# A group's update in three pieces and roots for three groups at once, in the weighted sum of a graph network kernel

## What is computed

```python
dst = (6250 * uniform(100000) ** 2.0).astype(int32)   # sorted; src is sorted along
edge_index = stack([src, dst])
h = maximum(_layernorm(x), 0.0)                       # (x - m) / sqrt(v + eps)
# attention, _L0: score from q[dst], k[src]; e = exp(score - smax[dst])
ssum = segment_sum(e, dst)
m = v[src] * attn[:, :, None]                         # attn = e / ssum[dst]
t = segment_sum(m, dst).reshape(N, DIM)
new_h = (t @ Wa + ba) * alpha + h * (1.0 - alpha)
x = x + new_h
h = maximum(_layernorm(x), 0.0)                       # input of the next layer
# _L1: four message layers; _L2: two convolutions; _L3: a linear layer with neighbours
```

## Time and profile before

| what | us |
|---|---|
| median of 3 runs | 10655.52 (10635.86 to 10660.82) |
| the profiled execution, its own time | 10607.1 |
| its span | 10605.0 |
| scores pass and what stands ahead of it | to about 1540 |
| weighted sum, to its last step's add | 1547 to 1901 |
| first gather of the next pass | 1922.88 |
| the seven later passes | the other 8682 |

### The profile page before, as it was taken

How to read it: one execution, slowest core, us unless ns; L and a number is a source line. 1 busy time by engine, 2 the same in 40 slices (tenths; PEclk the granted TensorE clock), 3 DMA queues, 4 the chain that set the end, 5 groups by cost and what they waited for, 6 DMA issues and landing times.

```text
span 10605.0 us, 107124 instructions
## 1 busy us (share of the span) xinstructions
PE 5675.4 (54%) x23750; PEld 3922.0 (37%) x23751; DVE 3028.2 (29%) x7366; ACT 949.0 (9%) x1767; POOL 6216.3 (59%) x6738
## 2 busy tenths in 40 slices
PE   3566637566775667656675666653334333333334
PEld 2333437333443334433343333333333333333234
DVE  3444577212221122312222122331122112231222
ACT  1111100111111111101111111110000000000000
POOL 3655536565555655466554655546666666656665
PEclk7566659777887788878788778875566556665666
DMA  5777755332323323233332323221111111111111
GB/s 167 218 219 218 203 139 155 90 88 82 85 75 86 87 82 85 79 85 87 83 83 75 88 81 81 77 59 45 47 49 48 46 46 49 48 46 46 47 49 47
DMA packets 796948, 945.08 MB, mean 89 GB/s; under 512 B 269045, under 2 KB 530448, under 8 KB 796302
## 3 DMA queue, kind: packets, MB, share of 16 engines
q0 software_dynamic: 213408, 463.35, 16.4%
q1 hardware_dynamic: 474970, 390.60, 13.2%
q10 hardware_dynamic: 108436, 89.99, 2.6%
HBM read 797.55 MB, written 152.25 MB: 90 GB/s over the span
## 4 chain that ended last, share of the span: by engine, by line
another core or an unknown queue 44%; PE 18%; issue 13%; DVE 9%; DVEq 3%; POOL 0%; SPq 0%; ACT 0%; DMA 0%; ACTq 0%; POOLq 0%
PE ps_big L1119 8%; PE ps_seg L1126 5%; DVE onehots L1715 2%; DVE sums L1746 2%; DVEq L453 1%; PE ps_seg L1197 1%; PE ps_big L1197 1%; PE ps_big L1063 1%; PE ps_t L1038 1%; DVE gate L1894 1%; DVE h_res L1898 0%; DVE group_stats L1783 0%; PE ps_seg L1063 0%; PE ps_big L987 0%
## 5 line engine op out<-in xcount | busy, mean ns | idle before, releaser
L871 POOL DMA_INDIRECT rows<-node_rows,idx_all x5488 | 5209.8, 949 | 3470.5 <-SPq L713 1590.0
L1119 PE MATMUL ps_big<-rows,ident 128*128 (+1 forms) x1960 | 1221.8, 709 | 1386.0 <-DVE onehots L1715 1249.5
L1746 DVE TENSOR_TENSOR sums<-sums,ps_seg 128x128 f32 x1342 | 385.5, 287 | 5141.3 <-remote 3368.8
L1126 PEld LDWEIGHTS ps_seg<-onehots 128*128 128x128 f32 x7840 | 1206.0, 223 | 899.0 <-issue 735.5
L1126 PE MATMUL ps_seg<-onehots 128*128 128x128 f32 x7840 | 1236.4, 309 | 260.6 <-issue 168.0
L1715 DVE SCALAR_TENSOR_TENSOR onehots<-ps_mm,away 128x512 f32<-128x512 f32 x1975 | 1349.3, 684 | 21.4 <-issue 13.8
L1197 PE MATMUL ps_seg<-rows,onehots 128*128 (+1 forms) x2952 | 613.8, 372 | 1235.4 <-DVE onehots L1715 595.8
L1119 PE MATMUL ps_big<-q_res,ident 128*128 (+1 forms) x1960 | 1153.9, 674 | 150.9 <-issue 123.0
L1119 PEld LDWEIGHTS ps_big<-rows,ident 128*128 128x128 f32 x1960 | 412.0, 224 | 2036.2 <-DVE onehots L1715 1461.7
L871 POOL DMA_INDIRECT sums<-kv_rows,idx_all x784 | 743.4, 948 | 548.2 <-SPq L711 281.2
L1197 PEld LDWEIGHTS ps_seg<-rows,onehots 128*128 128x128 f32 x2952 | 536.7, 272 | 1301.7 <-DVE onehots L1715 619.0
(11 more groups left out here) (215 smaller groups left out, 2974.4 us busy)
## 6 DMA issues: line engine op xcount, KB each, us to landing
q_res<-gates_by_edge SPq DMA_DIRECT2D x784, 256.0 KB
rows<-node_rows,idx_all POOLq DMA_INDIRECT x5488
rows<-dst_padded SPq DMA_DIRECT2D x196, 256.0 KB
value_rows_by_edge<-sums SPq DMA_DIRECT2D x196, 256.0 KB
gates_by_edge<-gate ACTq DMA_DIRECT2D x196, 256.0 KB
rows<-value_rows_by_edge SPq DMA_DIRECT2D x196, 256.0 KB, 3.5
node_rows<-h_res ACTq DMA_DIRECT2D x49, 448.0 KB
sums<-kv_rows,idx_all POOLq DMA_INDIRECT x784
```

The lines of the kernel that those rows point to most:

```text
L871: pool.indirect_dma_start(target[:, r, j, :], None, table, bass.IndirectOffsetOnAxis(ap=idx_all[:, c * J + j:c * J + j + 1], axis=0), elem ...
L1119: last = nc.tensor.matmul(ps_big[u][:, :], ident[:, :], chunk_words(source, slot, 0, CHUNK), start=n == 0, stop=n == 1)
L1126: last = nc.tensor.matmul(ps_seg[u][:, 0:D], onehots[:, u, j, :], msg[:, u, j, 0:D], start=j == 0, stop=j == J - 1)
L1746: V.tensor_tensor(mine, mine, seg_four[(n - 1) % depth][:, 0:D], ALU.add).then_inc(agg_added, 1)
```

## The change

`add_attention` moves from behind the third step to the end of the turn and keeps only the two additions. The statistics (`sample_attention`) go to the turn after, four windows behind the second step and three behind the third; `gather_attention` at that turn's end aggregates them into `mv`. The root and the shift are taken by `take_roots` when groups 0 to 2 are complete, then for 3 to 5, then for 6, each for up to 21 columns at once, into `rstd` and `nmr`. ACT normalises and stores group g-3 instead of g-1, so groups 3 to 6 are left for after its loop. DVE's word row has 10 words instead of 8, SP loads the table in 15 DMAs instead of 11, and each turn of DVE has five branches instead of three: behind the second and third step, and three at the end of the turn. `inverse_root` has 12 operations instead of 13 in all its uses.

```diff
-        SUM_WORDS, ROW_WORDS = 8, 12
+        SUM_WORDS, ROW_WORDS = 10, 12
-        WORD_LOADS = 11
+        WORD_LOADS = 15
+        ROOTS = ((0, 3), (3, 6), (6, 7))
...
+                    (sum_words[0:1, 0:1, 8:9], by_turn(ENDS_, 0, 1)[:, 0:1]),
+                    (sum_words[0:1, 1:TURNS_, 8:9], by_turn(ENDS_, 0, 1)[:, 0:TURNS_ - 1]),
+                    (sum_words[0:1, 0:1, 9:10], by_turn(ENDED_, 0, 1)[:, 0:1]),
+                    (sum_words[0:1, 1:TURNS_, 9:10], by_turn(ENDED_, 0, 1)[:, 0:TURNS_ - 1]),
...
-            def finish_and_store(g):
-                wait_alone(act, "act", deviation_ready, g + 1)
+            def finish_and_store(g, roots):
+                act.wait_ge(deviation_ready, roots + 1)
...
-                                                bias=group_nmr[:, i:i + 1], scale=group_rstd[:, i:i + 1])
+                                                bias=nmr[:, ds(g * GROUP + i, 1)], scale=rstd[:, ds(g * GROUP + i, 1)])
                 last.then_inc(group_done, 1)
-                wait_alone(act, "act", group_done, g + 1)
-                act.sem_inc(deviation_used, 1)
                 store_group(0, g, 0)
...
+            LATER = ROOTS[0][1]
             def attend_group(g):
-                with act.If(g != 0):
-                    finish_and_store(one_before(g, GROUPS))
+                with act.If(g >= LATER), clamped(act, [g - LATER], 0, LATER - 1) as earlier:
+                    finish_and_store(earlier[0], 0)
...
-            finish_and_store(GROUPS - 2)
+            finish_and_store(LATER, 1)
             copy_group(0, GROUPS - 1, copies_u)
-            finish_and_store(GROUPS - 1)
+            for g in range(LATER + 1, GROUPS - 1):
+                finish_and_store(g, 1)
+            finish_and_store(GROUPS - 1, 2)
...
-                do(V.tensor_scalar(v, x, add, None, ALU.add))
+                do(V.tensor_scalar(v, x, add, 0.5, ALU.add, ALU.mult))
                 do(V.tensor_single_scalar(t.bitcast(i32), v.bitcast(i32), 1, ALU.arith_shift_right))
-                do(V.tensor_scalar(y.bitcast(i32), t.bitcast(i32), -1.0, float(0x5F3759DF), ALU.mult, ALU.add))
-                do(V.tensor_scalar(v, v, -0.5, None, ALU.mult))
+                do(V.tensor_scalar(y.bitcast(i32), t.bitcast(i32), float(0x2108A621), -1.0, ALU.add, ALU.mult))
...
+            def sample_attention(g, first, end):
+                for i in range(first, end):
                     last = V.bn_stats(group_stats[:, i, :], win(x_res, g * GROUP + i))
+                last.then_inc(group_chain[0], 1)
...
+            def gather_attention(g):
+                wait_alone(dve, "dve", group_chain[0], g * OPS_ATT + 3)
                 for i in range(GROUP):
                     last = V.bn_aggr(group_mv[:, i, :], group_stats[:, i, :])
+                last.then_inc(group_chain[0], 1)
+                wait_alone(dve, "dve", group_chain[0], g * OPS_ATT + 4)
+                V.tensor_copy(mv[:, ds(g * GROUP, GROUP), :], group_mv[:, :, :]).then_inc(group_chain[0], 1)
+            def take_roots(n):
+                a, b = (ROOTS[n][m] * GROUP for m in range(2))
+                do = Chain(dve, att_roots, n * OPS_ROOT)
+                dve.wait_ge(group_chain[0], ROOTS[n][1] * OPS_ATT)
+                inverse_root(do, rstd[:, a:b], mv[:, a:b, 1], EPS, root_all[:, 0, a:b], root_all[:, 1, a:b])
+                V.scalar_tensor_tensor(nmr[:, a:b], mv[:, a:b, 0], -1.0, rstd[:, a:b], ALU.mult, ALU.mult)\
                     .then_inc(deviation_ready, 1)
+            def finish_attention(g):
+                gather_attention(g)
+                for n, (_, end) in enumerate(ROOTS[:-1]):
+                    with dve.If(g == end - 1):
+                        take_roots(n)
...
-                    if n == 3:
-                        with dve.If(words[4] != 0), clamped(dve, words[5:6], 0, GROUPS - 1) as group:
-                            add_attention(group[0])
+                    if n == 2 or n == 3:
+                        with dve.If(words[8] != 0), clamped(dve, words[9:10], 0, GROUPS - 1) as group:
+                            sample_attention(group[0], *STATS[n - 2])
                 with dve.If(words[4] != 0), clamped(dve, words[5:6], 0, GROUPS - 1) as group:
+                    add_attention(group[0])
+                with dve.If(words[8] != 0), clamped(dve, words[9:10], 0, GROUPS - 1) as group:
                     finish_attention(group[0])
```

More of the change, by code:

```diff
@@ L141, in build_program @@
         part = sb("part", [P, 2, FH])
-        group_nmr = sb("group_nmr", [P, GROUP])
-        group_rstd = sb("group_rstd", [P, GROUP])
         attr_t = sb("attr_t", [P, 2, P])
@@ L323, in build_program @@
         deviation_ready = sem("deviation_ready")
-        deviation_used = sem("deviation_used")
+        att_roots = sem("att_roots")
         node_in_ready = sem("node_in_ready")
@@ L369, in build_program @@
         GROUPS = WINDOWS // GROUP
+        ROOTS = ((0, 3), (3, 6), (6, 7))
+        assert ROOTS[-1][1] == GROUPS
         def wait_alone(eng, name, semaphore, value):
@@ L1451, in inverse_root @@
                     do(V.tensor_tensor(t, t, v, ALU.mult))
-                    do(V.scalar_tensor_tensor(y, t, 1.5, y, ALU.add, ALU.mult))
+                    do(V.scalar_tensor_tensor(y, t, 1.5, y, ALU.subtract, ALU.mult))
             dve.wait_ge(dst_loaded, 96)
@@ L1798, in _ @@
             OPS_NORM = OPS_STATISTICS + 1
-            OPS_ATT = 1 + OPS_STATISTICS
+            OPS_ATT = 5
+            STATS = ((0, 4), (4, 7))
             def start_attention(g):
@@ L1820, in add_attention @@
                 dve.sem_inc(node_finished, 1)
-                for i in range(GROUP):
+            def sample_attention(g, first, end):
+                for i in range(first, end):
                     last = V.bn_stats(group_stats[:, i, :], win(x_res, g * GROUP + i))
-                do(last, alone=True)
-            def finish_attention(g):
-                do = Chain(dve, group_chain[0], g * OPS_ATT + 2)
+                last.then_inc(group_chain[0], 1)
+            def gather_attention(g):
+                wait_alone(dve, "dve", group_chain[0], g * OPS_ATT + 3)
                 for i in range(GROUP):
                     last = V.bn_aggr(group_mv[:, i, :], group_stats[:, i, :])
[L1829 to L1834, removed]
-                    .then_inc(deviation_ready, 1)
-                assert 2 + do.n == OPS_ATT
+                last.then_inc(group_chain[0], 1)
[7 more added lines that the diff above has]
+                V.scalar_tensor_tensor(nmr[:, a:b], mv[:, a:b, 0], -1.0, rstd[:, a:b], ALU.mult, ALU.mult)\
+                    .then_inc(deviation_ready, 1)
+                assert do.n == OPS_ROOT
+            def finish_attention(g):
[3 more added lines that the diff above has]
+                        take_roots(n)
             def attend_steps(i, words):
@@ L1867, in _ @@
                 mark_step(n * J, n)
-            each_turn(dve, "dve", sum_words, slice(0, 8), attend_steps)
+            each_turn(dve, "dve", sum_words, slice(0, 10), attend_steps)
+            regs = [dve.alloc_register(f"dve_last_{next(load_no)}")]
+            dve.load(regs, sum_words[0:1, TURNS_ - 1:TURNS_, 4:5].rearrange("a i n -> a (i n)"))
+            with dve.If(dve.snap(regs[0], donate=True) != 0):
+                for part_ in STATS:
+                    sample_attention(GROUPS - 2, *part_)
+                gather_attention(GROUPS - 2)
+                take_roots(1)
+            for r in regs:
+                dve.free_register(r)
             add_attention(GROUPS - 1)
-            finish_attention(GROUPS - 1)
+            for part_ in STATS:
+                sample_attention(GROUPS - 1, *part_)
+            gather_attention(GROUPS - 1)
+            take_roots(2)
             inverse_root(chain, dinv[:, :], agg[:, :, D + HEADS], 1.0, root_all[:, 0, :], root_all[:, 1, :])
```

3 lines of the change are left out of this document (1 added, 2 removed).

## The result

The changed kernel took 10780.08 us, the median of four runs (10758.14 to 10783.53), against 10649.92 for the kernel before, also of four (10635.86 to 10660.82): a ratio of 1.0125, with a 95% interval of 1.0102 to 1.0148. It is slower by about 133 us, where I forecast 10651 and gave a range up to 10682. The profiled execution took 10783.17 us; its span is 10781.4. Of the kernels further down, the last one (a_packed_sp) had two slow executions among its ten, of 16.43 and 16.68 ms at granted clocks of 0.34 and 0.31 where the other eight had 0.72; they are left out of its ratio, and what they were is open.

The account below looks back on a forecast made before the run. Weighted-sum turns were taken as bound by DVE, with its sequencer at each turn's end, and near POOL's pace in the first 21. Terms -20 + 13 + 5 - 3 + 0.5 = -4.5 us gave 10651, range 10608 to 10682.

Parts of the forecast that it names:

- part 2: End of every DVE turn in the weighted sum: one more branch and two more words loaded, 13 us more (4 to 28).
- the rule of 200 ns a register: Trainium skill's price for bulk register loads: two more DVE words 0.4 us; the prediction said it doesn't hold here.
- The first rival: DVE's turn end in the weighted sum: its sequencer pays 0.46 us in all 61 turns, +10 us, 10666; chance 0.22.
- Part 1: Group update in the weighted sum, done in pieces with fewer roots: 20 us less (10 to 30).
- the third rival: Group turns of the weighted sum: the stall vanishes, only roots are left, -46 to -49 us, 10608; chance 0.10.
- the fourth: Group turns: DVE still stops as long for PE, the update in pieces gives only 10 us, +6, 10661; chance 0.13.
- the second rival: Branches within DVE's steps aren't hidden: 25 us more than the turn's end deciding, 10691; chance 0.05.
- Part 3: SP's queue ahead of the weighted sum: four more table DMAs, 5.3 us, cost 5 us more (0 to 5.3).
- Part 4: Roots of later passes: one operation less in each, mostly hidden behind gathers, 3 us less (0 to 8.4).
- Part 5: ACT behind the weighted sum's loop: groups 4 and 5 normalised there too, 0.5 us more (-0.5 to 4.4).

Follow-up runs that it names:

- a_packed_sp: Changed kernel with flag and group packed in one word, DVE rows of eight words, and SP's table in rows of eight: 0.9975 of the kernel before.
- b_pe_off: Kernel before with two unused words between DVE's and PE's tables, so only PE's rows start off a multiple of 16 bytes: 1.0131 of the kernel before.
- b_row10: Kernel before with DVE's table rows ten words long, still loading eight: 1.0175 of the kernel before.
- b_dve_off: Kernel before with DVE rows of ten words and a two-word gap, so only each second DVE row starts off 16 bytes: 1.0048 of the kernel before.
- a_packed: Changed kernel with flag and group packed in one word, DVE rows of eight words, twelve table DMAs: 10574.36 us, 0.9975 of the kernel before.
- a_load12: Changed kernel with DVE rows padded to twelve words and all twelve loaded, the last two unused: 0.9989 of the kernel before.
- a_row12: Changed kernel with DVE rows padded from ten to twelve words, two never loaded: 10502.72 us, 0.9991 of the kernel before.
- b_costs: Kernel before with twelve-word DVE rows, ten words loaded, fifteen table DMAs and two more branches a turn, update in one piece: 1.0024 of the kernel before.

## Why the prediction was wrong

**The step that failed is in part 2**: "two cost between 0.03 and 0.25, and I take 0.2". I priced two more words by their number, from PE's rows of 8 and 12 words. All of those start at a multiple of 16 bytes, so they could show neither the price of ten words (1.07, 0.47 more, as the last two come singly) nor that of a row that starts off it (2.30, 1.7 more). And I costed the load that the diff adds to, not the one that it moves: PE's table starts where DVE's ends. Its load went from 0.85 to 2.87 us, and that makes three quarters of the loss (b_pe_off against b_row10). My sentence that the rule of 200 ns a register doesn't hold for this table was true of the rows that I had; in the kernel that I predicted PE's load takes 239 ns a word. By that rule I had made the part 12 us dearer; by b_row10 a wrong start costs 184 us in the kernel before (0.0175 of 10509). A row against it lay in the trace of before: SP's load of eight words at 1.67 us beside DVE's of eight at 0.60. Two prices for the same instruction were a question that I didn't ask, since SP's isn't on the path.

**What bounds an ordinary turn of the kernel before** was read rightly. The gap at its end is DVE's own sequencer: the shortest one is 1.60 us in b_dve_off (load 0.60), 1.80 in a_packed (the same load, one branch more), 2.07 at a load of 0.86 (a_load12) and 2.29 at 1.07 (a_row12). The first rival, *the turn's end decides*, had DVE's end of the turn and a price of 0.46 us, where the loads brought 0.47 to 1.70 on DVE and 2.02 on PE. No rival had PE's sequencer as the bound. I had given PE 3.8 us of matmuls in a turn and left it at that; it is busy for 4.0 of 4.35, and could not take in 2.02 us more.

**Part 1**, the update in pieces, held: 18.7 us against 20 (a_row12 against b_costs). The turns of groups were forecast at 8.2 and 7.9 us; group 0's in a_row12 are 8.64 (1638.45 to 1647.09) and 7.92:

```profile
1638.45 0.30 DVE L1872 TENSOR_TENSOR sums<-sums,ps_seg 128x137 f32 x1 [0.81 <-issue]
...
1642.47 0.30 DVE L1872 TENSOR_TENSOR sums<-sums,ps_big 128x137 f32 x1 [1.52 <-PE ps_big L1067]
1643.29 1.26 DVE L1823 SCALAR_TENSOR_TENSOR x_res<-ps_t,alpha,x_res 128x512 f32 x2
1647.09 0.30 DVE L1872 TENSOR_TENSOR sums<-sums,ps_seg 128x137 f32 x1 [2.54 <-issue]
1648.71 0.86 DVE L1831 BATCH_NORM_STATS2 group_stats<-x_res 128x6 f32 x4
...
1652.48 0.17 DVE L1841 COPY mv<-group_mv 128x14 f32 x1 [0.25 <-DVE group_mv L1838]
1655.01 0.30 DVE L1872 TENSOR_TENSOR sums<-sums,ps_seg 128x137 f32 x1 [2.35 <-issue]
```

The fourth add waits for PE, 4.0 us into the turn instead of 4.7, and the issue time behind the additions is longer than I had it. The two turns with roots (11.27 and 11.19) are 3.3 us longer than the others (7.91), where I took 4.5. So the third rival, *the stall vanishes*, and the fourth, *it stops as long*, are both out.

**Part 2 with the start put right**: 19.5 us (b_costs; the DMAs lie before that stretch) against 13. The load brought 0.47 instead of 0.2. The branch at the end brought 0.2 as forecast (1.80 against 1.60 above), and those within the steps nothing: most steps, with and without one, take 0.80 to 0.82 us in the changed kernel. That puts out the second rival, at any address.

**Part 3**: the four DMAs took 1.8 us, not 5.3, and POOL stood 11.10 instead of 6.79 us behind SP's queue, though its first gather came only 1.7 us later, 19.3 instead of 17.6 us after the first of them. What that did to the start of the weighted sum can't be told: it began at 1543.4 us against 1547.1, but with eleven DMAs it began anywhere from 1516 to 1547 in these profiles. **Part 4**: 13 us by the middle of an interval from 0 to 26, against 3; where it would be isn't known. **Part 5**: no wait that can be seen, against 0.5.

Put together for a kernel whose rows start right, my sum was -4.5 us; a_row12 measured -9 (0.9991, from -20 to +1). The terms of the edit were near enough, in part by luck: part 2 was 6.5 us too small, part 3 about 3 too large by the DMAs' own time, and part 4 isn't settled. What decided was the address of a table that the edit pushed along.

## What to carry to other kernels

A load of words into registers is priced by its start as well as by its number: keep rows of such a table, and the start of every table behind it in the same tile, at a multiple of 16 bytes, and fill a row up to a multiple of four words (twelve are cheaper than ten). When an edit widens a row, list what lies behind it and look again at the instructions that read that, even on engines that the diff doesn't touch. When the same instruction shows two durations anywhere in a trace, find out what sets them before one is used as a price.

## What the runs showed of the hardware

- Loads of words from SBUF into registers take, at a multiple of 16 bytes from the tile's start, 0.60 us for 8 words and 0.85 for 12, so 0.25 for four more, and 1.07 for 10, so 0.23 or 0.24 for each of two single ones; off it, 0.23 to 0.24 a word throughout (1.86 for 8, 2.30 for 10, 2.87 for 12). Two words took 0.49 on ACT in both kernels. Only offsets of 8 bytes were tried on DVE and PE. SP's eight words took 1.67 us (0.21 a word) at 4, 8 and 12 bytes off alike, and 0.53 in each fourth turn.
- A busy sequencer's price stands in the trace under other names: at DVE's first adds the profile put the time down to "issue" or to PE, and at PE's resumed matmuls to POOL, whose operation had ended 0.36 us before, though the weight loads there resume at a nearly fixed distance (0.50 to 0.64 us) from the end of PE's load.
- An untaken branch at the end of a DVE turn cost 0.2 us (gaps of 1.80 and 1.60 us in a_packed and b_dve_off), and one within a step cost nothing, behind a one-hot block of 0.68 us.
